# Turning the attention outputs by a transposing DMA instead of on TensorE

## The reference

```python
Q = phi(xn @ Wq + bq); K = phi(xn @ Wk + bk); V = xn @ Wv + bv    # phi(z) = elu(z) + 1; 16 heads of 64
KV = KV + k_i v_i^T; Ks = Ks + k_i                                # causal: over the tokens of a batch
out_i = (q_i KV) / (q_i . Ks + 1e-6); attention = out @ Wo + bo
gate = sigmoid((xn @ tree_Wq.T) @ routers.T)                      # 255 nodes, depth 8
tree = (leaf_probs(gate) @ leaf_values) @ Wout_w.T + Wout_b       # 256 leaves
```

## Time and profile before

| what | value |
|---|---|
| median of three runs | 1233.66 us (1233.03 to 1235.53) |
| the profiled execution, its own time | 1235.54 us |
| its span, first to last instruction | 1233.8 us |
| granted TensorE clock, mean | 0.994 |
| busy: PE / PEld / DVE / ACT / POOL | 97% / 85% / 66% / 45% / 55% |
| DMA queue q1, share of 16 engines | 21.8% |

### The profile page before, as it was taken

How to read it: one execution, slowest core, us unless ns; L and a number is a source line. 1 busy time by engine, 2 the same in 40 slices (tenths; PEclk the granted TensorE clock), 3 DMA queues, 4 the chain that set the end, 5 groups by cost and what they waited for, 6 DMA issues and landing times.

```text
span 1233.8 us, 48282 instructions
## 1 busy us (share of the span) xinstructions
PE 1202.1 (97%) x21669; PEld 1052.3 (85%) x21669; DVE 811.4 (66%) x2186; ACT 551.7 (45%) x881; POOL 675.5 (55%) x842
## 2 busy tenths in 40 slices
PE   5899999999999999999999999999999999999987
PEld 4789889898988989889898988989889898988967
DVE  4774876757667574875758667574866758667462
ACT  3553552535445253552535445253552535445251
POOL 3475556455554665556455554655556465554550
PEclk9999999999999999999999999999999999999998
DMA  6121211212123121222213122121222213122120
GB/s 230 20 53 36 57 34 45 54 36 54 36 46 53 37 54 36 57 34 45 54 36 54 36 46 53 36 54 36 55 36 45 53 36 54 36 45 36 37 36 19
DMA packets 154654, 58.94 MB, mean 48 GB/s; under 512 B 134081, under 2 KB 152784, under 8 KB 154448
## 3 DMA queue, kind: packets, MB, share of 16 engines
q1 hardware_dynamic: 154448, 55.86, 21.8%
HBM read 14.43 MB, written 8.39 MB: 18 GB/s over the span
## 4 chain that ended last, share of the span: by engine, by line
PE 95%; DVE 2%; ACT 1%; POOL 1%; DMA 1%; issue 1%; SPq 0%; POOLq 0%; DVEq 0%
PE s_pair L705 26%; PE w_pair L705 22%; PE o_pair L717 9%; PE s_pair L717 9%; PE o_pair L814 6%; PE s_pair L778 5%; PE o_pair L828 5%; PE kv_pair L789 5%; PE w_pair L758 5%; PE w_pair L740 2%; DMA ffn_tok<-in_L_ffn_Wout_w_dram 1%; ACT ex L455 0%; ACT ex L458 0%; PE o_pair L705 0%; DVE wk L250 0%
## 5 line engine op out<-in xcount | busy, mean ns | idle before, releaser
L353 POOL TENSOR_SCALAR_AFFINE_SELECT aT<-aT 64x512 f32<-64x512 f32 x256 | 167.7, 655 | 366.0 <-ACT aT L482 357.1
L482 ACT ACTIVATE aT<-s_pair 128x512 f32<-128x512 f32 x128 | 76.4, 597 | 337.6 <-PE s_pair L778 337.6
L705 PE MATMUL w_pair<-xnT,wk 128*128 128x512 f32 x768 | 212.3, 412 | 4.1 <-ACT k_tok L468 2.2
L705 PE MATMUL s_pair<-xnT,wq 128*128 128x512 f32 x756 | 200.9, 401 | 1.4 <-POOL aT L353 1.1
L632 DVE TENSOR_TENSOR snaps<-kv_pair,snaps 128x65 f32<-128x65 f32 x768 | 173.3, 226 | 26.5
L404 POOL COPY k_tok<-k_turned 128x1024 uint16<-128x1024 uint16 x126 | 171.4, 1361 | 29.6 <-POOL aT L353 22.6
L396 POOL COPY k_planes<-kT 128x1024 uint16<-128x1024 uint16 x126 | 131.2, 1041 | 95.1 <-POOL k_tok L404 58.2
L455 ACT ACTIVATE ex<-w_pair,neg_bias 128x512 f32<-128x512 f32 x130 | 89.6, 689 | 189.5 <-PE w_pair L705 189.5
L705 PE MATMUL s_pair<-wv,xnT 128*128 128x512 f32 x648 | 168.5, 394 | 0.1
L458 ACT ACTIVATE ex<-ex 128x512 f32<-128x512 f32 x256 | 161.9, 633 | 8.1
L705 PEld LDWEIGHTS w_pair<-xnT,wk 128*128 128x128 f32 x768 | 134.4, 188 | 36.2 <-ACT k_tok L468 2.7
(11 more groups left out here) (107 smaller groups left out, 1972.1 us busy)
## 6 DMA issues: line engine op xcount, KB each, us to landing
x_in<-in_L_attn_x_dram SPq DMA_DIRECT2D x16, 512.0 KB, 5.1
out_dram<-y_buf SPq DMA_DIRECT2D x32, 256.0 KB, 2.1
k_turned<-k_planes SPq DMA_TRANSPOSE x126, 3.1
stage<-in_L_attn_Wv_dram SPq DMA_DIRECT2D x2, 512.0 KB, 8.0
stage<-in_L_attn_Wk_dram SPq DMA_DIRECT2D x2, 512.0 KB, 9.6
stage<-in_L_attn_Wq_dram SPq DMA_DIRECT2D x2, 512.0 KB, 10.9
stage<-in_L_attn_Wo_dram SPq DMA_DIRECT2D x2, 512.0 KB, 9.4
bv_all<-in_L_attn_bv_dram SPq DMA_DIRECT2D x1, 512.0 KB, 8.6
```

Source lines behind the costliest of these rows:

```text
L353: pool.affine_select(out=part, in_=part, compare_op=ALU.is_ge, fill=0.0, base=0, pattern=[[0, 2 * CH], [1, D]], channel_multiplier=-1).the ...
L482: act.activation(aT[:, n % 2].rearrange("p h c q -> p h (c q)"), s_pair[:, :, 0:CH * D], ACT.Copy).then_inc(s_copied, 1)
L705: last = pe.matmul(dst, l, r, start=i == 0, stop=i == len(steps) - 1)
```

## The change

For 109 of the 128 units (all but p = 7 of each block and the first three units) the outputs no longer go through TensorE's transposes. GpSimd splits `o_tok` into two planes (`take_output_apart`), SP issues a transposing DMA (`turn_output`), ScalarE joins the planes to `o_full` and rounds the high part one unit later, before it takes up the keys (`put_output_together`, `high_of_turned`), and VectorE subtracts from SBUF (`low_of_turned`), after `phi` of the keys and before the other fills. VectorE runs `norm(n)` before `carry(n + 1)`. Head fills go to S1 and tails to W1. TensorE waits at other places: for V at the outer product that needs it, for O0 and O1 at the first matmul in each, for `k_whole` only at the outer products, for `o_normed` before Q's last matmul. The halves of every odd chunk of 128 tokens are swapped in `x_in` and in the stored rows, for which each load of x is three DMAs and each store of a block six in place of two.

```diff
+def by_dma(n):
+    return n % PAIRS < PAIRS - 1 and n >= 3
...
     fills = [(("K", keys[1], keys[0]), W0)] if keys else []
-    fills += [(name, W1) for name in head]
+    fills += [(name, S1) for name in head]
     if queries:
         fills.append((("Q", queries[1], queries[0]), S0))
-    fills += [(name, S1) for name in tail]
-    fills.append((("oT", p, g), W1))
+    fills += [(name, W1) for name in tail]
     if p == PAIRS - 1:
-        fills += [(("y", 0, g), O1), (("y", 1, g), S1)]
+        fills += [(("oT", p, g), W1), (("y", 0, g), O1), (("y", 1, g), S1)]
+    elif not by_dma(n):
+        fills.append((("oT", p, g), S1))
...
+            def load_block(g):
+                dst, src, done = x_in[:, g % 2], x_rows[g], x_loaded[g % 2]
+                sp.dma_start(dst[:, 0::2], src[:, 0::2]).then_inc(done, 16)
+                sp.dma_start(dst[0:D, 1::2], src[D:P, 1::2]).then_inc(done, 16)
+                sp.dma_start(dst[D:P, 1::2], src[0:D, 1::2]).then_inc(done, 16)
...
+            def turn_output(n):
+                g, p = divmod(n, PAIRS)
+                sp.wait_ge(o_apart, units_by_dma(n))
...
+                sp.dma_start_transpose(o_turned(p), o_planes.rearrange("p s n -> p (s n)")).then_inc(o_turned_in, 16)
...
                 if p == 0 and g:
                     store(g - 1)
+                if by_dma(n):
+                    turn_output(n)
                 if n + 3 < UNITS:
                     turn_keys(n + 3)
...
+            def take_output_apart(n):
+                k = units_by_dma(n)
+                pool.wait_ge(o_normed, n + 1)
+                if k > 1:
+                    pool.wait_ge(o_turned_in, 16 * (k - 1))
+                pool.tensor_copy(o_planes, o_tok[:, :, :, :].rearrange("p b t n -> p (b t n)").bitcast(U16)
+                                 .rearrange("p (n s) -> p s n", s=2)).then_inc(o_apart, 1)
...
                 if n + 1 < UNITS:
                     mask(n + 1)
+                if by_dma(n):
+                    take_output_apart(n)
...
+            def put_output_together(n):
...
+                act.activation(o_full[:, 1, p].bitcast(U16).rearrange("p (n s) -> p s n", s=2),
+                               o_turned(p).rearrange("p (s k) q -> p s (k q)", s=2), ACT.Copy).then_inc(o_whole, 1)
+            def high_of_turned(n):
+                g, p = divmod(n, PAIRS)
+                act.wait_ge(o_whole, units_by_dma(n))
+                act.activation(oT[:, 0, p], o_full[:, 1, p], ACT.Copy).then_inc(oT_hi, 1)
...
                     copy_scores(n + 1)
+                if n and by_dma(n - 1):
+                    put_output_together(n - 1)
+                    high_of_turned(n - 1)
...
+            def low_of_turned(n):
+                g, p = divmod(n, PAIRS)
+                dve.wait_ge(oT_hi, n + 1)
+                dve.tensor_tensor(oT[:, 1, p], o_full[:, 1, p], oT[:, 0, p].bitcast(F32), ALU.subtract)\
+                   .then_inc(o_low, 1)
...
+                norm(n)
                 if n + 1 < UNITS:
                     carry(n + 1)
-                norm(n)
...
+                turned = n and by_dma(n - 1)
+                for name in values_first([name for name, _ in unit_fills(g, p, BLOCKS)], p):
                     kind, i, b = name
+                    if turned and kind != "K":
+                        low_of_turned(n - 1)
+                        turned = False
...
-                if p in (0, HALF):
-                    for c in reversed(range(CH)):
-                        until_drained((f"V{p // HALF}", c, g))
                 outer_products(n)
```

More of the change, by code:

```diff
@@ L25, with units_by_dma @@
 W0, W1, S0, S1, O0, O1 = range(6)
+def by_dma(n):
+    return n % PAIRS < PAIRS - 1 and n >= 3
+def units_by_dma(n):
+    return sum(by_dma(m) for m in range(n + 1))
 def unit_fills(g, p, blocks):
@@ L155, in attention_and_tree_layer, with o_turned @@
         k_turned = sb("k_turned", [P, 2 * CH, P], U16)
+        o_planes = leaf_odd.rearrange("p c n -> p (c n)").bitcast(U16).rearrange("p (s n) -> p s n", s=2)
+        def o_turned(p):
+            place = gate if p < HALF else xn
+            return place[:, 2 * (p % 2):2 * (p % 2) + 2].rearrange("p c n -> p (c n)").bitcast(U16)\
+                .rearrange("p (k f) -> p k f", f=P)
         aT = sb("aT", [P, 2, 2, CH, D])
@@ L164, in attention_and_tree_layer @@
         with nc.sbuf_tensor("stage", [P, 4, KT_ * inner], F32) as stage:
+            pass
+        with nc.sbuf_tensor("o_full", [P, 2, PAIRS, TOK], F32) as o_full:
             pass
@@ L608, in norm @@
                 dve.wait_ge(den_step, 2 * n + 2)
+                if n and by_dma(n - 1):
+                    dve.wait_ge(o_apart, units_by_dma(n - 1))
                 dve.tensor_tensor(o_tok[:, :, :, :].rearrange("p b t (h e) -> p b (t h) e", e=D), v[:, :, :, 0:D],
@@ L688, in _ @@
                         output(name)
+                if turned:
+                    low_of_turned(n - 1)
         @block.tensor
@@ L713, in output_rows @@
                     for t in Y_TILES:
+                        if c == 0 and t in (0, PAIRS - 2):
+                            until(o_low, units_by_dma(g * PAIRS + max(t, PAIRS - 3)))
                         if c == 0 and t == PAIRS - 1:
@@ L739, in fill @@
                     for c in range(CH):
-                        last = pe.transpose(dst[:, c * P:(c + 1) * P], src[:, c, i * P:(i + 1) * P], ident[:, :])
+                        to = dst[:, c * P:(c + 1) * P].rearrange("p (a q) -> p a q", a=2)
+                        to = to[:, ::-1] if c % 2 else to
+                        last = pe.transpose(to, src[:, c, i * P:(i + 1) * P], ident[:, :])
                 elif kind == "gate":
@@ L755, in fill @@
                     for c in range(CH):
-                        to = dst[:, c * P:(c + 1) * P].rearrange("p (a q) -> p a q", a=2)
-                        last = pe.transpose(to[:, ::-1] if c % 2 else to, o_tok[:, c % 2, c // 2], ident[:, :])
+                        last = pe.transpose(dst[:, tile_of_output(c)], o_tok[:, c % 2, c // 2], ident[:, :])
                 else:
@@ L782, in outer_products @@
             def outer_products(n):
-                p = n % PAIRS
+                g, p = divmod(n, PAIRS)
                 half = p // HALF
                 for t in range(CH):
+                    if p in (0, HALF):
+                        until_drained((f"V{half}", t, g))
                     for a in range(2):
@@ L807, in from_state @@
                     h = t % 2 ^ turn
+                    if turn == 0 and t < 2:
+                        until(drained[(O0, O1)[t]], uses_before[n][(O0, O1)[t]])
                     for a in range(2):
@@ L864, in tiled @@
                 if n >= 0:
-                    for bank in (O0, O1):
-                        until(drained[bank], uses_before[n][bank])
                     until(sum_ready, sums_after[n])
@@ L935, in _, with normed, head_ready @@
                 fills = unit_fills(n // PAIRS, n % PAIRS, BLOCKS)
-                first_by_vector = any(bank == W1 and name[0] in ("V1", "xT", "leaf") for name, bank in fills)
+                def normed():
+                    until(o_normed, n + 1)
+                def head_ready():
+                    for kind, i, g in (f for f, _ in fills):
+                        if kind == "xT":
+                            until(xn_ready, g + 1)
+                        if kind == "leaf" and i == 0:
+                            until(leaf_step, (g + 1) * LEVEL_STEPS)
                 def masked():
@@ L941, in masked @@
                         until(a_masked, 2 * n + 4)
-                def whole():
-                    if n + 2 < UNITS:
-                        until(k_whole, n + 1)
                 for name, bank in fills:
@@ L957, in _ @@
                             until_drained(("xT", t, g))
-                    if kind == "leaf" and i == 0:
+                    if kind == "leaf":
                         until(leaf_step, (g + 1) * LEVEL_STEPS)
@@ L962, in _ @@
                             until_drained(("leaf", t, g))
-                    fill(name, masked if kind == "Q" else whole if bank == S1 and kind != "y" else None)
+                    fill(name, head_ready if kind == "K" else normed if kind == "Q" else masked if bank == W1 and kind in ("V0", "V1") else None)
                     if kind == "y" and i == 0:
-                        whole()
+                        masked()
+                normed()
                 masked()
-                whole()
 _INS = ['L0_attn_x', 'L0_attn_Wq', 'L0_attn_bq', 'L0_attn_Wk', 'L0_attn_bk', 'L0_attn_Wv', 'L0_attn_bv',
```

48 lines of the change are left out of this document (32 added, 16 removed).

## The result

The changed kernel takes 1239.61 us (median of 6 runs, 1238.94 to 1241.34), the kernel before beside it 1233.91 (6 runs, 1231.95 to 1235.58): a ratio of 1.0047 with an interval of 1.0034 to 1.0060. It is slower by half a per cent, and 109 times four transposes are gone. The profiled execution takes 1240.21 us with a span of 1238.5, 4.7 more than the 1233.8 before.

What follows compares the result with a forecast made beforehand. TensorE's matmul time, 95% of the chain, was taken as the bound. Blocks summed to +2.4 us and transfers and last block to +1.5: +3.9 on the profiled 1235.54, a median of about 1238, range 1211 to 1263.

Steps and rivals of the forecast that it cites:

- The sum of +3.9: Whole kernel: +2.4 us from 16 blocks and +1.5 from transfers and last block, added to the profiled 1235.54.
- The subtraction from SBUF: VectorE's subtraction waits for GpSimd's joining over shared ports, ends at 4.83; p = 1, 3, 4 take 7.22, -0.18 each.
- the faster rival: GpSimd's 16-bit copies don't hold VectorE up; p = 1, 3, 4 take 7.04, about 1215 us in all; chance 0.25.
- The sign that I had named: In the profile after, VectorE's subtraction has a mean near 1.0 to 1.3 us instead of 0.68, longest in p = 2.
- `residual` and p = 2: GpSimd's `residual` runs 1.0 us into p = 2, delaying joining and subtraction; next K at 8.47, +1.03.
- p = 0 and normalising first: VectorE normalising before the sums is hidden in all units but p = 0, which takes 8.45, +0.10.
- ScalarE's copy: ScalarE's joining of the planes takes 1.06 us; 1.4 would cost nothing, as the port binds first.
- The transposes at 0.36: The outputs' transposes cost 0.36 us of TensorE's stream per unit, 39 us over 109 units.
- "If nothing waits": Without waits on TensorE, units p = 1, 3, 4 take 7.04 us and p = 5 7.95.
- The turned data in time: Each transposing DMA lands 3.1 us after issue; both turns of a unit are hidden, with 1.3 us to spare.
- the late case: Slower rival: turns always land in 5.0, GpSimd 0.6 later in p = 0 to 4, 1286 us; chance 0.05.
- The ends: Loads and stores at both ends and the last block's lighter units, about 0.5 us each, together +1.5.

Runs made afterwards that it cites:

- e1: Changed kernel with VectorE's subtraction from SBUF put ahead of `phi` of the keys: 1255.64 us, ratio 1.0187 to the kernel before.
- e2: e1 with the subtraction's first operand read from the keys' bank of PSUM (low parts wrong, same work): 1225.63 us, ratio 0.9944 to the kernel before.
- e3: Changed kernel with ScalarE's copy writing 1024 contiguous 16-bit elements, without the stride (values wrong): 1239.22 us, ratio 1.0054 to the kernel before.
- e5: Changed kernel with GpSimd's `residual` and the load of x in p = 6 instead of p = 1 and 2: 1233.98 us, ratio 1.0009 to the kernel before.
- e6: Changed kernel with the sums again ahead of the normalising on VectorE: 1256.42 us, ratio 1.0188 to the kernel before.
- e4: Changed kernel with the edits of e2 and e3 together (values wrong): 1208.51 us, ratio 0.9815 to the kernel before.
- e10: Changed kernel, outputs' joining, rounding and subtraction later, e5's edit, output rows' wait for unit 5's low part moved to its tile: 1217.98 us, 0.9876 of kernel before.
- e11: Kernel before without the outputs' transposes and their high and low parts in 105 units, nothing in their place: 1231.10 us, ratio 0.9995.
- e12: Changed kernel with one load of x and two stores a block, as before (odd chunks' rows misplaced): 1237.14 us, ratio 1.0041 to the kernel before.
- e9: Kernel before with e5's edit (`residual` and the load of x in p = 6): 1231.62 us, ratio 0.9988.

## Why the prediction was nearly right, and where it was not

The forecast, about 1238 and slower, was right: 1239.61. The sum of +3.9 stands against +4.7 in the profiled spans and +5.7 in the medians, but much of that agreement is luck: errors cancel in the sum (the late turns against the ends and p = 5), and in the usual unit too.

**The subtraction from SBUF: a real wait, but not what sets the usual unit.** That VectorE waits for GpSimd over SBUF is shown: e1 and e2 differ by the place of one operand and by 30 us, and the two units of e1 show each engine held by the other, whichever came second. The rule of the Trainium skill, page "SBUF — State Buffer", section "SBUF: two separate sides", which I had weighed, is that whichever of the two starts first has the shared ports for its whole instruction; the traces agree: with two operands in SBUF a subtraction that meets GpSimd's operation ends 0.49 behind it, and with one in PSUM it takes 692 ns whatever GpSimd does. So the faster rival fell as it was put, that the port is no obstacle. But in the kernel after, the subtraction of a usual unit p = 1, 3 or 4 takes 0.68 and waits for nobody. It ends at 4.83 as forecast because ScalarE's copy is 0.31 longer than I took it, while GpSimd alone would have let it end at 4.78 (e3). Two limits 0.05 apart, one of them mis-sized: the 7.23 for the 7.22 worked out is luck. The sign that I had named, a mean of 1.0 to 1.3 us, came in p = 2 (1.25) and not in the whole (829 ns). What the port does cost in this kernel lies in p = 2 and in the units with late keys, some 13 us by the ratios of e2 and of the kernel after.

**`residual` and p = 2: right in size** (8.41 for 8.47). Of its +0.97 over the kernel before, 0.46 goes when `residual` goes elsewhere (e5) and 0.56 when the subtraction needn't wait (e2), which is the same wait twice; some 0.4 stays in both, with the subtraction still ahead of xT, the values and `phi` of Q. It is the dearest single term of a block.

**p = 0 and normalising first: right** (8.46 for 8.45). That it is "hidden" elsewhere was too little said: e6 shows that it is needed.

**ScalarE's copy: wrong in size.** I took 1.06; it takes 1.37, the 1.4 that I had noted as costing nothing "as the port binds first". In a usual unit it doesn't: with 1.37 it is the copy that lets the subtraction end last, by 0.05. That it costs only 0.03 a unit (e3) is right all the same, and e4 shows that it matters once the wait for GpSimd is gone.

**The transposes at 0.36: mis-sized, and for the wrong reason.** The 0.36 came from a place where full-size matmuls follow. In p = 1, 64x64 tiles follow: from the values' product to the first state product it was 360.08 - 358.16 = 1.92 before, and is 1.49 in e10. The two stretches:

```profile
358.16 1.55 PE L705 MATMUL s_pair<-wv,xnT 128*128 128x512 f32 x6
359.55 0.60 PE L758 MATMUL w_pair<-ident,o_tok 128*128 128x128 f32 x4
360.08 0.40 PE L814 MATMUL o_pair<-snaps,qT 64*64 64x65 f32 x11
```

```profile
353.58 1.55 PE L806 MATMUL w_pair<-wv,xnT 128*128 128x512 f32 x6
355.07 0.40 PE L928 MATMUL o_pair<-snaps,qT 64*64 64x65 f32 x11
...
357.08 1.67 PE L806 MATMUL w_pair<-xnT,wk 128*128 128x512 f32 x6
```

That is 0.43. Another 0.14 lies between the state products and the next K (362.23 - 360.08 = 2.15 before, 357.08 - 355.07 = 2.01 in e10), where the scores of the kernel before reach their bank about when the values leave it. Together 0.57, and the units differ by 7.40 - 6.84 = 0.56. So p = 1, 3, 4 can take 6.84, in units in which TensorE waits for nobody, and not 7.04, and p = 5, in which TensorE waits for nobody after the change, gains 0.53 a block where I had 0.36. And the step had a hidden condition, the bank: with the banks as before the removal is worth 0 (e11), and in e10, with the swap and all else of the change, 0.56 in such a unit. "If nothing waits" was written over a bank that does wait.

**The turned data in time: the step that failed.** I counted 3.1 for each turn, 1.3 us to spare, and gave the late case a chance of 0.05 as if it came always or never. It came in part. Of the 19 long units, 15 follow a turn of the keys of over 4.1 us in the unit before (9 in p = 0, 6 in p = 3). In two more, p = 4 of blocks 10 and 13, ScalarE waits 0.3 for the outputs' turn. The other two add 0.3 us together, and I have no cause for them. The means of p = 1 and p = 4 lie 0.34 and 0.20 over their usual length, +0.54 a block, 7.6 us in all, of which the late keys are 6.5. Without this excess the blocks would take 74.07, as long as before (74.07), where I had +0.13.

Two numbers of that step were wrong. The landing: the earlier trace rows had 5.0 as the longest, and the median of 3.1 hides that 31 of the 126 took over 4 us already before. And the time to spare: the keys' turn is issued 5.75 into p = 3, as counted (5.7), but 7.25 into p = 0, where `phi` of K stands behind the normalised rows. It then lands 1.9 into p = 1 at best, and GpSimd is free for it at 2.87: 1.0 us to spare in place of 1.3. That is why p = 1 and p = 4 are the ones that grow, though turns are late in units of every p: the joining in p = 2 comes late anyway, behind `residual`; p = 3 has the long p = 2 before it; and in p = 5 and p = 6, of mean length 7.80 and 8.35, a later subtraction does little.

Late keys cost by way of the subtraction that waits for the late joining, and in e2, where it waits for nothing, they cost nothing in p = 1. What makes a turn take 4.9 stays open: it isn't the loads and stores (e12) nor `residual` (e5), it is there without the outputs' turns (31 before), and in the case shown no other turn was under way, as the outputs' was issued 4.35 earlier, at 348.73.

**The ends: not what I had, and mostly not to be told.** I had +1.5 for the transfers at both ends and the last block, and +0.15 for each of the two blocks there, +1.8; in the two profiled executions they came to -3.0. Half of that lies before the K of unit 0 (43.36 and 41.83). Among the profiles of the runs this K stands anywhere from 40.26 (e12) to 44.36 (e3), and at 40.67 in e9, which differs from the kernel before only later on: a difference of 1.5 there is no effect of the change. Block 0 gives -0.8, as some units grow (7.40 to 7.98) and others shrink (8.87 to 8.00, 7.40 to 6.83), which I had not looked at one by one; the last block and the end give -0.7. By the medians, +5.7, the ends come to about -2. So blocks 1 to 14 were 5.6 worse than forecast (+7.7 for +2.1), and the ends some 4 to 5 better, part of it by the accident of which executions were profiled. That the terms sum up near zero is no law: e10 makes the same transfers and is 1.2% faster than the kernel before, e1 is 1.9% slower.

## What to carry to other kernels

Before you count what a shorter stream gives, ask of each bank and buffer in it who would be late if the work were not there: the chain may say 95% and the gain be zero. Work that moves to VectorE should keep one operand in PSUM while GpSimd is busy in SBUF; where it can't, put it where nobody waits for it, one unit later if need be. Take the longest landing of a DMA, not the median, for a hand-over with little to spare, work out what is to spare in each kind of unit, and count how often it would miss. A time that comes out as forecast doesn't show its cause: look whether the instruction that should have waited is longer than it is alone.

## What the hardware did that I had not expected

- ScalarE's copy of 1024 halves of 16 bits written with a step of two takes 1372 ns, written in a row 1050 (e3). GpSimd's takes 1.35 and 1.04: nearly the same pair.
- The wait for the SBUF works both ways, and the order of start decides within 0.02 us: GpSimd's joining takes 1.36, and 1.90 when VectorE's subtraction is just ahead of it (e1). Its splitting has a mean of 1300 ns in the kernel after, where the subtraction is under way when it starts, and 1042 in e1, where it is over.
- A good part of the turns of the keys take 4.0 to 5.0 us for 3.1: 31 of 126 before, 44 of 126 after. Their cause was not found.
